# Set-up of an adaLN attention and LoRA-expert kernel: the first attention rows start on four tiles while the other four are prepared

## The reference

```python
mod = (_silu(L0_c) @ L0_wmod).reshape(L0_c.shape[0], 6, 1, -1)
sa, ca, ga, sb, cb, gb = (mod[:, 0], mod[:, 1], mod[:, 2], mod[:, 3], mod[:, 4], mod[:, 5])
ga = (2 * (ga >= 0) - 1) * jnp.maximum(jnp.abs(ga), 0.25)
gb = (2 * (gb >= 0) - 1) * jnp.maximum(jnp.abs(gb), 0.25)
h = _layernorm(x, axis=-1) * (1 + ca) + sa
x = x + ga * _L0_attn_ref(h, ...)      # layer norm with gamma, beta; causal attention, one head of 256; + residual h
h = _layernorm(x, axis=-1) * (1 + cb) + sb
x = x + gb * _L0_ffn_ref(h, ...)       # router, top 2 of 8 experts, each a rank-16 LoRA on a SwiGLU of width 704
```

## Time and profile before

| | |
|---|---|
| median of 3 runs | 670.13 us (669.81 to 670.28) |
| the profiled execution's own time | 669.96 us |
| its span in the trace | 668.1 us |
| PE busy | 652.1 us, 98% of the span, 3890 instructions |
| DVE, ACT, POOL busy | 466.5, 360.3, 369.5 us (70%, 54%, 55%) |
| chain that ended last | PE 84%, DVE 10%, ACT 3%, the rest below 2% each |
| mean granted clock of PE | 0.997 |

### The profile page before, as it was taken

How to read it: one execution, slowest core, us unless ns; L and a number is a source line. 1 busy time by engine, 2 the same in 40 slices (tenths; PEclk the granted TensorE clock), 3 DMA queues, 4 the chain that set the end, 5 groups by cost and what they waited for, 6 DMA issues and landing times.

```text
span 668.1 us, 10913 instructions
## 1 busy us (share of the span) xinstructions
PE 652.1 (98%) x3890; PEld 561.4 (84%) x3890; DVE 466.5 (70%) x1146; ACT 360.3 (54%) x646; POOL 369.5 (55%) x442
## 2 busy tenths in 40 slices
PE   8799999999999999999999999999999999999996
PEld 6488987888889987888889897887889998798885
DVE  5857676888785776688776677689886757547323
ACT  1766466545555547555455446564455456654543
POOL 1099366538658236657676317665666525633644
PEclk9999999999999999999999999999999999999999
DMA  8400020000000020000000001000000000000000
GB/s 308 138 1 1 2 64 0 1 1 32 0 1 32 1 65 1 0 1 33 0 1 32 1 6 59 1 1 33 1 0 27 7 1 1 1 1 1 32 0 33
DMA packets 15032, 15.47 MB, mean 23 GB/s; under 512 B 1793, under 2 KB 13697, under 8 KB 14977
## 3 DMA queue, kind: packets, MB, share of 16 engines
q1 hardware_dynamic: 14976, 14.76, 6.6%
HBM read 10.57 MB, written 4.19 MB: 22 GB/s over the span
## 4 chain that ended last, share of the span: by engine, by line
PE 84%; DVE 10%; ACT 3%; issue 1%; DMA 1%; POOL 0%; SPq 0%; DVEq 0%; ACTq 0%
PE ps L1265 78%; PE ps L1274 6%; DVE hid L1112 2%; DVE rstd L844 1%; DVE zb L864 1%; DMA xs<-in_L_attn_x 1%; DVE neg_mean L1176 1%; ACT xr L587 1%; ACT act_s L725 1%; DVE zb L867 0%; DVE stat L998 0%; DVE stat L861 0%; DVE topi L1057 0%; DVE xr L1007 0%; DVE nr_a L842 0%
## 5 line engine op out<-in xcount | busy, mean ns | idle before, releaser
L475 POOL TENSOR_TENSOR ring_lo<-hid,ring_hi 128x512 fp32r<-128x512 f32 x144 | 187.2, 1304 | 110.0 <-ACT ring_hi L733 109.4
L725 ACT ACTIVATE act_s<-ps 128x512 f32<-128x512 f32 x120 | 71.6, 597 | 123.0 <-PE ps L1265 122.4
L1112 DVE TENSOR_TENSOR hid<-act_s,ps 128x512 f32<-128x512 f32 x120 | 82.1, 684 | 78.9 <-ACT act_s L725 74.1
L733 ACT ACTIVATE ring_hi<-hid 128x512 fp32r<-128x512 f32 (+1 forms) x144 | 90.4, 627 | 5.3 <-PE ps L1265 3.5
L1265 PE MATMUL ps<-wdT_hi,ring_hi 128*128 128x256 f32 x192 | 53.2, 283 | 0.0
L1265 PE MATMUL ps<-wdT_lo,ring_hi 128*128 128x256 f32 x192 | 52.7, 280 | 0.0
L467 POOL TENSOR_TENSOR xT_lo<-tr_full,xT_hi 128x512 fp32r<-128x512 f32 x28 | 35.9, 1297 | 29.0 <-ACT xT_hi L597 29.0
L1265 PE MATMUL ps<-wdT_hi,ring_lo 128*128 128x256 f32 x160 | 44.7, 280 | 0.0
L1265 PE MATMUL ps<-vv_hi,pT_hi 128*128 128x256 f32 x144 | 42.9, 298 | 0.1
L1265 PE MATMUL ps<-tm_hi,bgT_hi 128*128 128x512 f32 x96 | 39.5, 411 | 2.4 <-DVE hid L1112 2.4
L482 POOL TENSOR_TENSOR xr<-xr,y_gb 128x256 f32<-128x256 f32 x31 | 22.6, 754 | 33.6 <-DVE y_gb L1147 33.6
(11 more groups left out here) (232 smaller groups left out, 2018.2 us busy)
## 6 DMA issues: line engine op xcount, KB each, us to landing
out<-xr SPq DMA_DIRECT2D x7, 512.0 KB, 2.9
xs<-in_L_attn_x SPq DMA_DIRECT2D x3, 1024.0 KB, 5.7
xs<-in_L_attn_x SPq DMA_DIRECT2D x2, 512.0 KB, 4.7
s_mod<-in_L_wmod SPq DMA_DIRECT2D x2, 512.0 KB, 7.6
s_qkvT<-in_L_attn_qkv SPq DMA_DIRECT2D x1, 768.0 KB, 7.4
wgT_raw<-in_L_ffn_Wg SPq DMA_DIRECT2D x1, 704.0 KB, 7.9
wuT_raw<-in_L_ffn_Wu SPq DMA_DIRECT2D x1, 640.0 KB, 8.7
wdT_raw<-in_L_ffn_Wd SPq DMA_DIRECT2D x1, 640.0 KB, 5.7
```

What stands on the lines that cost most here:

```text
L475: pool.tensor_sub(ring[1][:, place(n), :], hid[:, n % HID, :], ring[0][:, place(n), :].bitcast(fp32)).then_inc(h_lo.sem, 1)
L725: nc.scalar.activation(act_s[:, n % 2, :], ps[:, 2 * (n % 2), :], ACT.Silu).then_inc(silu_ready.sem, 1)
L733: nc.scalar.activation(ring[0][p0:P, place(n), :], hid[p0:P, n % HID, :], ACT.Copy).then_inc(h_hi.sem, 1)
L1112: V.tensor_mul(hid[:, n % HID, :], act_s[:, n % 2, :], ps[:, 2 * (n % 2) + 1, :]).then_inc(h_ready.sem, 1)
```

## The change

Only set-up and the body of batch 0 are changed; later batches keep their order.

1. *Two chunks apart.* PE transposes tiles 0 to 3, makes the two `queries` of the first chunk and row 0's scores, then `values` of tiles 0 to 3 and row 1's scores; only then it transposes tiles 4 to 7. The other two `queries` are in row 2 and the values of tiles 4 to 7 in row 3. ACT's `first_normalise` of tiles 4 to 7 is at the start of row 0. The functions `proj_place`, `proj_bank` and `turn_bank` give order and banks for batch 0.
2. *DVE.* The first Newton rounds have `ln1_centre` of tiles 0 to 3 between them, for which ACT copies the scale first (`first_scale`). The clamping of the gates moves into the Newton rounds of the first chunk, and the work on tiles 4 to 7 that stood in them moves behind `first_shifts(0)`.
3. *Modulation.* Scale jobs 1 to 3 are one matmul each with 4 partitions (`batch_rows`, `scale_rows`) in place of two with 128; a `mod_row(0)` makes their rows. The gates are spread for batch 0 first (`spread_gates(0, 1)`), then for the rest. The last two gate jobs are in row 1.
4. *Unread matmuls.* 28 matmuls of 128 columns stand ahead of the first `queries`.
5. *POOL and ACT.* `wvo` waits for the first chunk's shift alone, the residuals still for the second's. ACT makes all high parts of weights in rows 2 to 6. POOL makes 7 of the 12 low parts ahead of the Newton rounds, 2 (`bgT`, `buT`) behind them and 3 (`wdT` twice, `adT`) behind `tr_low` of the first FFN chunk. PE's wait is split likewise: 6 before the router, 9 before the adapters, 12 before the first down product.
6. *ACT's table.* An exponential whose result is not read stands right after the silu of `c`.

The diff, cut to its core:

```diff
-        BODY_HIGH = {0: (4, 5, 6), 1: (7,), 2: (8,), 3: (9,), 4: (10,), 5: (11,)}
+        BODY_HIGH = {2: (0, 1), 3: (2, 3, 4), 4: (5, 6, 7), 5: (8, 9, 10), 6: (11,)}
...
+        FIRST_PROJ = (0, 1, 4, 5, 2, 3, 6, 7)
+        FIRST_PROJ_BANKS = (0, 1, 1, 3, 4, 5, 1, 3)
+        FIRST_TURN_BANKS = (0, 1, 1, 3)
+        W_ROUTER, W_UP = 6, 9
...
-            pool.wait_ge(first_shift, 2)
+            pool.wait_ge(first_shift, 1)
             values_weight(0)
             values_weight_low(0)
             pool.wait_ge(wvo_lo.sem, wvo_lo.at(0, 0))
+            pool.wait_ge(first_shift, 2)
             for i in range(NT):
...
-            for j in range(WEIGHT_STEPS):
+            for j in range(W_ROUTER + 1):
                 weight_low(j)
...
+                if b == 0:
+                    for j in range(W_ROUTER + 1, W_UP):
+                        weight_low(j)
                 for k in range(KT):
                     tr_low(b, KT * NC + k, [t[:, 0, k, :] for t in xT])
+                if b == 0:
+                    for j in range(W_UP, WEIGHT_STEPS):
+                        weight_low(j)
...
+                    if b == 0 and i == 0:
+                        act.wait_ge(first_shift, 2)
+                        for tile in range(TC, NT):
+                            first_normalise(tile)
...
+            for i in second:
+                ln1_centre(0, i)
+            wqk_low()
+            settle()
             dve.wait_ge(loaded["ln"], 32)
             attention_scale(0, range(KT))
+            for i in second[:2]:
+                first_rows(i)
             for q in range(KT):
                 attention_low(q)
+            for i in second[2:]:
+                first_rows(i)
+            for i in second:
+                first_stats(i)
+            queries_values(0, (0,))
+            moments(second)
+            mark(guess(TC, TC, True))
+            queries_values(0, (1,))
...
+                elif what == "scale":
+                    last_mm = mm(ps[:, bank, :], batch_rows[:, b, :], scale_rows, True, True)
...
+            for _ in range(28):
+                mm(ps[:, 2, 0:P], identb[:, :], identb[:, :], True, True)
+            queries(0, (0, 1))
+            pe.wait_ge(gates_spread, 2)
+            modulation(5)
...
-                            pe.wait_ge(proj_lo.sem, proj_lo.at(b, 3))
+                            pe.wait_ge(proj_lo.sem, proj_lo.at(b, proj_place(b, 3 if b else 1)))
...
+                        if b == 0 and i == 0:
+                            values(b, range(NT // 2))
+                        if b == 0 and i == 1:
+                            attention_transposes(b, 1, [xr[:, t, :] for t in range(TC, NT)])
+                            pe.wait_ge(modT_copied, 1)
+                            modulation(6)
+                            modulation(7)
+                        if b == 0 and i == 3:
+                            values(b, range(NT // 2, NT))
...
+                    if b == 0 and i == 2:
+                        queries(b, (2, 3))
```

More of the change, by code:

```diff
@@ L572, in modulation @@
                 act.wait_ge(mod_ready, job + 1)
-                if what == "scale":
+                if job == 0:
+                    nc.scalar.activation(bc[:, b, CA, :], ps[:, MOD_BANKS[job], D:2 * D], ACT.Identity, bias=1.0).then_inc(first_scale, 1)
+                    nc.scalar.activation(bc[:, b, SA, :], ps[:, MOD_BANKS[job], 0:D], ACT.Copy).then_inc(mod_copied, 1)
+                elif what == "scale":
                     nc.scalar.activation(bc[:, b, SA, :], ps[:, MOD_BANKS[job], 0:D], ACT.Copy).then_inc(unwaited, 1)
@@ L940, in _ @@
             moments(range(NT))
-            rsqrt(0, NT)
+            mark(guess(0, NT))
+            settle()
+            for n, small in enumerate(first_newton(0, NT)):
+                mark(small())
+                at = steps[1]
+                if n == TC:
+                    dve.wait_ge(first_scale, 1)
+                if TC <= n < 2 * TC:
+                    ln1_centre(0, n - TC)
+                dve.wait_ge(vstep, at)
             dve.wait_ge(mod_copied, 1)
-            for i in first:
-                ln1_centre(0, i)
             settle()
@@ L962, in _ @@
                 mark(small())
-                at = steps[1]
-                if n < len(big):
-                    big[n]()
-                dve.wait_ge(vstep, at)
+                if n == 3:
+                    dve.wait_ge(gates_turned, 1)
+                for clamp in clamps.get(n, ()):
+                    mark(clamp())
+                if n == 6:
+                    V.scalar_tensor_tensor(g, gate_sign[:, :], -1.0, gate_size[:, :], ALU.add, ALU.mult).then_inc(gates_made, 1)
+                settle()
             first_shifts(0)
             for i in second:
-                first_stats(i)
-            moments(second)
-            link(guess(TC, TC, True))
-            for small in first_newton(TC, TC):
-                link(small())
-            first_shifts(TC)
+                ln1_centre(0, i)
+            wqk_low()
+            settle()
             dve.wait_ge(loaded["ln"], 32)
             attention_scale(0, range(KT))
+            for i in second[:2]:
+                first_rows(i)
             for q in range(KT):
                 attention_low(q)
-            attention_scale(0, range(KT, KT * NC))
-            for q in range(KT, KT * NC):
-                attention_low(q)
-            dve.wait_ge(modT_copied, 1)
-            V.tensor_scalar_add(modT[:, 1, :, :], modT[:, 1, :, :], 1.0).then_inc(modT_made, 1)
-            dve.wait_ge(modT_made, 1)
-            queries_values(0, range(6))
+            for i in second[2:]:
+                first_rows(i)
+            for i in second:
+                first_stats(i)
+            queries_values(0, (0,))
+            moments(second)
+            mark(guess(TC, TC, True))
+            queries_values(0, (1,))
+            settle()
+            for n, small in enumerate(first_newton(TC, TC)):
+                mark(small())
+                if n == 0:
+                    dve.wait_ge(modT_copied, 1)
+                    mark(V.tensor_scalar_add(modT[:, 1, :, :], modT[:, 1, :, :], 1.0))
+                settle()
+            first_shifts(TC)
             setup_steps = steps[1]
@@ L1015, in body @@
                         V.tensor_reduce(rowmax[:, i:i + 1], banks[:, 0:w], X, ALU.max, negate=True).then_inc(rowmax_ready.sem, 1)
+                    if b == 0 and i == 0:
+                        queries_values(b, (4,))
+                    if b == 0 and i == 1:
+                        attention_scale(b, range(KT, KT * NC))
+                        for q in range(KT, KT * NC):
+                            attention_low(q)
+                        queries_values(b, (5,))
+                    if b == 0 and i == 3:
+                        queries_values(b, (6, 7))
                     if 3 <= i < 3 + TC - 1:
```

197 lines of the change are left out of this document (113 added, 84 removed).

## The result

| | before | after |
|---|---|---|
| median (range, runs) | 670.38 us (669.73 to 671.09, 20) | 671.33 us (670.41 to 673.59, 20) |
| ratio, 95% interval | | 1.0017 (1.001 to 1.0024) |
| profiled execution: time, span, clock | 669.96, 668.1 us, 0.997 | 673.59, 671.8 us, 0.992 |

The changed kernel is slower by 0.17%. That is inside the 0.2% that I had called no change, but the interval does not touch 1, and the forecast had been a small gain (669.6). The range of 667.4 to 671.9 held the time, but not by merit of the sum, whose own range ended at 670.6: it reached further because it allowed for a slower DVE and for one fall of the clock, in another place and for another reason. The profiled execution of after is the slowest of its 20 runs.

What follows compares the result with a forecast made beforehand. PE was taken to bound the kernel, so only its gaps, clock and instruction count matter. From 669.96 us, minus 2.0 in set-up, plus 1.65 before the masks, gave 669.6 us; eight-in-ten range 667.4 to 671.9.

Steps and rivals of the forecast that it cites:

- the sum: Whole kernel: set-up gain of 2.0 us and router loss of 1.65 us give 669.6 us; own range 668.8 to 670.6.
- What bounds the kernel: Whole kernel: PE busy 98% of the span; time comes only from PE standing still, running slowly or having fewer instructions.
- The schedule of set-up: Set-up to row 2's probability transposes: PE reaches them at 52.0 instead of 54.04, gaining 2.0 us (0.4 to 2.8).
- Both meetings of DVE with POOL: Second chunk: DVE's rows wait beside `wvo_lo`, costing 0.75 us; its low parts take 2.33 us beside POOL's residuals.
- DVE's queue takes more (C): Set-up: POOL wins the first meeting too, gain only 0.4 us, time 671.2 us; chance 0.15.
- The late low parts: Router before the masks: `wdT` and `adT` on POOL delay DVE's `lg` and `pr`; PE loses 1.65 us (0 to 3.6).
- Rival A: Router: the late low parts do no harm, time 668.0 us; chance 0.25.
- the scale jobs: Set-up modulation: one matmul on 4 partitions takes 0.94 us against 1.88 for two; the saving falls ahead of a wait.
- granted clock 1.0 throughout: Sign of a right forecast: PE's clock never falls; a clock of 0.5 behind a gap would show it wrong.
- Rival B: New PE gaps of 2.15 us at 42 and 1.65 before the masks lower the clock, 1.5 us each: 672.6 with both; chance 0.15.

Runs made afterwards that it cites:

- e2: Changed kernel with the three late scale jobs reading 128 partitions of other data instead of 4 (scale of batches 1 to 3 not the reference's): 669.50 us, ratio 1.0003.
- e4: Changed kernel with POOL making the low parts of both `wdT` ahead of `xT_lo`, only `adT` behind it: 670.17 us, ratio 0.9996.
- e1: The changed kernel run once more without any edit: 671.15 us, ratio 1.0016.
- e3: Changed kernel without the 28 unread matmuls ahead of the first queries: 671.72 us, ratio 1.0023.
- e5: Changed kernel with the three scale jobs on 128 partitions, 124 of them zeros, result as the reference's: 670.72 us, ratio 1.0002.
- e10: e9 without the 28 unread matmuls: 667.18 us, ratio 0.9952.
- e8: e6 with all POOL residuals held until DVE has made the second chunk's low parts, and without the 28 unread matmuls: 669.29 us, ratio 0.9984.
- e6: Changed kernel with the edits of e5 and e4 together: 669.43 us, ratio 0.9985.
- e9: e6 with POOL making three residuals at once and the other five after DVE's second low parts: 667.36 us, ratio 0.9952.

## Why the prediction was wrong

**What bounds the kernel** was right: time moved only through PE's gaps, and through its clock.

**The schedule of set-up was right at full clock.** `e2` is its test: transposes 23.20 (forecast 23.4), gap 0.28 (0.5), queries 28.23 (28.6), gap 1.23 (1.5), gap 2.09 ending at 43.84 (2.15, at 44.3), mark 51.53 (52.0). Both meetings of DVE with POOL went as said, with durations 1.91 and 2.40 (forecast 2.0 and 2.33). From the first product to the mark it is 2.2 us shorter than before (2.0 in the sum). Its span, 667.1, is 1.0 us below before, where the sum had 0.35, but 0.3 of that is the shorter warm-up and owes nothing to the kernel. The rival that DVE's queue takes more (C) is thereby out: the lateness of after is not on DVE.

**The late low parts** were right in mechanism, place and sign, and a little too dear: 1.21 us at DVE and 1.20 at PE (`e4` against `e1`) for a forecast of 1.65. The part that was off is `lg`: it waited 0.22 us, not 0.7. The kernel met it later relative to `wdT_lo` than I had placed it: `lg` began 3.25 us behind that operation's start, and I had it 2.93 behind; and I counted its delay from its start to POOL's end, while it ends together with POOL's operation. Rival A, no harm, is refuted. The Trainium skill (SBUF — State Buffer, section "SBUF: two separate sides") says that the pair of ports goes to one engine for a whole instruction. By that rule, the traces agree: DVE's 32-column steps end within 0.06 us of the end of POOL's operation, and take 0.19 us when POOL is silent (`e4`).

**The step that failed is the scale jobs.** I wrote that one matmul on 4 partitions costs "between nothing and half" of the old pair, took 0.94 us "because the columns that stream are the same", and put "granted clock 1.0 throughout" among what would show the forecast right. The duration was right: the job takes as long with 4 rows as with 128 (1.96 us for two in `e3`, 1.98 in `e2`). The Trainium skill (TensorE: Matmul & The Clock Gate, section "Why this matters for your kernels") says that a lone matmul with a contraction of 32 takes the same time as one of 128; the traces agree for 4. But the clock did not stay, although in after PE had next to no gap. With 128 rows, of other data (`e2`) or of zeros (`e5`), and nothing else changed on PE, it stayed at 1.00. That is shown by the profiled executions: of the four with 4 rows (after, `e1`, `e3`, `e4`) each has a fall that begins between 26 and 30 us, of the seven with 128 rows (`e2`, `e5` to `e10`) none. The other runs have no trace, but their mean clocks agree: none of the 50 runs with 4 rows is above 0.997, and 51 of the 68 with 128 rows are at 0.998 or more. In the medians, full rows bring the kernel from 1.0016 of before (`e1`) to 1.0003 and 1.0002 (`e2`, `e5`), level with before and still not below it, since part of their runs are in the upper groups. In `e3` the fall comes with a gap of 1.54 us, so there the gap may have a share; but `e8` and `e10`, with a gap of 1.2 us in that place and full rows, keep the clock.

The price follows from the rows, counted from the first product, which stands 0.44 us later in after than in `e2` for the warm-up alone. In after, the unread matmuls and the queries run to 34.65 instead of 31.06, 3.6 us later; the shorter wait for `qT_lo` (0.77, not 1.23) gives back 0.46, and the wait ahead of the transposes of row 1's probabilities ends at 46.98 instead of 43.84, 3.14 later. Without the 0.44 the first fall costs 2.7. From there to the mark it is 9.22 us in after and 7.69 in `e2`: the second fall costs 1.53. Together they cost this run, the slowest of its 20, 4.2 us. In `e1`, with one shorter fall, the way from the first product to the mark is 1.1 longer than in `e2`.

In `e1`, which is nearer to the median run, the parts are, against before: 2.2 us gained up to the mark at full clock, 1.1 lost to the fall, 1.06 to the late low parts and 0.3 behind the masks. That is a loss of some 0.2 us where the sum had a gain of 0.35. The other 0.8 of the 1.0 us between the two spans is the longer warm-up of `e1`.

**Rival B** (the clock falls in the new gaps; slower) was nearest, and I gave it 0.15. It asked only what a gap does, and so missed the fall that had no gap in front of it. Of its two gaps the one of 2.0 to 2.1 us is borne out in part: in after and `e4` the clock fell behind it, in `e1`, `e2`, `e3`, `e5` and `e6` it did not. It then costs the 1.53 us above, as B's 1.5 said. The gap ahead of the masks, 1.25 us in the end, lowered it in no trace.

**What stays open.** That the upper groups of `e2`, `e5` and `e6`, 2.2 to 2.4 us above the lower in their medians, are runs in which the 2 us gap lowered the clock is an inference. For it: a lower mean clock in them, and no such group once the gap is 1.0 us (`e9`, `e10`, five runs each). Against it: only one execution of each kernel has a trace, and none of those three shows a fall; in `e5` the groups' clocks, 0.997 and 0.998 to 1.000, are close together; and the distance is more than the 1.53 us that the fall costs in after. A longer warm-up in the same runs could make up the difference (it varies by 1.6 us over the traces), but no trace shows it. It would take a trace of a run of the upper group. Why the warm-up takes longer in one execution than in another is open too. The gain of `e9` over `e6`, 1.8 us in the profiled spans, can be read without that: neither of the two traces has a fall, the shorter gap is 1.0 of it, and 0.7 is the warm-up (7.71 us, not 8.41), which is luck.

## What to carry to other kernels

When a matmul with many rows is replaced by one with few, count not only its columns: look at the granted clock behind it, because PE can be busy all the time and still be slowed; filling the idle partitions with zeros cost nothing here and kept the clock. Unread matmuls put in as cover run at the clock that is granted, so when they are too many for the low clock they become the delay. When work of POOL is moved, look at which two-input operations of DVE it now meets, in both places: here two low parts made earlier and one wait among the residuals were worth 2.2 us (`e5` to `e9`: 1.2 from mark to masks, 1.0 ahead of the mark), as much as the whole rearrangement of set-up gained up to the mark. And before the ends of two traces are compared, compare their starts: the same warm-up differed by up to 1.6 us.

## What the runs showed of the hardware

With the scale jobs on 4 rows the clock fell to 0.50 in them or within 0.6 us of their end in all four traces, with PE busy in three of the four; on 128 rows in none of seven, and 124 rows of zeros held it as well as data did. A gap of 1.96 to 2.09 us lowered the clock in two of seven traces of equal shape, so a single trace does not tell how such a gap ends; the spread of the runs tells more. The same 110 warm-up matmuls took 7.55 to 9.15 us in twelve traces. DVE's operations on two SBUF tensors took longer beside a POOL operation: 1.18 us in place of 0.19 in the router, with the end 0.06 us behind POOL's, and 2.41 in place of 1.42 for two low parts.
